# A branch hint for the back edge at the head of every turn of the loops of an image model's kernel

## The reference

```python
out = L0_conv(x)        # 8 heads of 12 channels with rotary positions:
attn = jax.nn.softmax(jnp.einsum('bhnd,bhmd->bhnm', q * scale, k), axis=-1)   # 2304 x 2304 a head
out = jnp.einsum('bhnm,bhmd->bhnd', attn, v)
# L1_conv: a Fourier filter (rfft2, two complex block matrices, irfft2)
# L2_attn: attention with one head of all 192 channels
# L2_ffn:  eight experts, each token to one of them, with a capacity
# L3_attn: retention, 12 heads of 16 channels:
retention = jnp.einsum('mhsd,mhtd->mhst', q, k) * decay
out = jnp.einsum('mhst,mhtd->mhsd', retention, v) + k
# L3_ffn:  jnp.einsum('bsi,oi->bso', x, jnp.sign(weight))
```

## Time and profile before

| | |
|---|---|
| median of 3 runs | 7712.14 us (7709.46 to 7726.1) |
| profiled execution | 7705.95 us |
| its span, first to last instruction | 7704.4 us |
| TensorE matmuls busy | 6614.5 us, 86% |
| VectorE busy | 4720.3 us, 61% |
| ScalarE busy | 3174.2 us, 41% |
| GpSimd busy | 2305.7 us, 30% |
| granted clock of TensorE, mean | 0.907 |

### The profile page before, as it was taken

The page is one execution under the profiler, slowest core; times in us unless marked ns, Lnnn a source line. Parts: engine busy times, 40 slices in busy tenths (PEclk is TensorE's granted clock), DMA queues, the critical chain, the costliest instruction groups (busy, mean ns, idle before and its releaser), DMA issues. The chain is left out here.

```text
span 7704.4 us, 233323 instructions
## 1 busy us (share of the span) xinstructions
PE 6614.5 (86%) x87595; PEld 4183.7 (54%) x87595; DVE 4720.3 (61%) x7714; ACT 3174.2 (41%) x5336; POOL 2305.7 (30%) x2558
## 2 busy tenths in 40 slices
PE   6698999999997677599999982499779999999977
PEld 4254555555554554276767672377445555555546
DVE  6688888888883400132323236011579999999976
ACT  2066666767674133122222220122344444444432
POOL 0011111111111000000000000300339999999961
PEclk8699999999998788699999985799889999999986
DMA  3211111111113423301010012211651111111123
GB/s 116 76 38 38 35 38 36 38 37 38 37 33 79 121 59 92 97 1 28 1 28 19 1 53 83 74 54 42 190 176 37 38 36 37 37 37 38 36 64 105
DMA packets 415540, 428.73 MB, mean 56 GB/s; under 512 B 76977, under 2 KB 387801, under 8 KB 409659
## 3 DMA queue, kind: packets, MB, share of 16 engines
q1 hardware_dynamic: 332859, 339.62, 15.4%
q0 software_dynamic: 62400, 59.16, 3.1%
q10 hardware_dynamic: 19712, 21.53, 0.9%
HBM read 253.47 MB, written 166.55 MB: 55 GB/s over the span
## 5 line engine op out<-in xcount | busy, mean ns | idle before, releaser
L628 DVE TENSOR_REDUCE softmax_part_max<-softmax_ring 128x1 f32<-128x512 f32 (+1 forms) x2880 | 1679.3, 632 | 333.9 <-PE softmax_ring L536 276.2
L2456 POOL TENSOR_TENSOR retention_decayed<-retention_third,retention_decay_table 128x384 f32<-128x384 f32 x1728 | 1690.5, 1005 | 106.1 <-ACT retention_third L2478 101.6
L2437 DVE TENSOR_TENSOR retention_decayed<-retention_scores,retention_decay_table 128x768 f32<-128x768 f32 x1728 | 1654.1, 957 | 89.9 <-PE retention_scores L2398 57.5
L668 ACT ACTIVATE softmax_probs<-softmax_scores 128x768 f32<-128x768 f32 x1728 | 1392.4, 810 | 676.4 <-PE softmax_scores L558 604.1
L536 PE MATMUL softmax_ring<-softmax_k_next,softmax_q_next 96*32 96x512 bf16 (+1 forms) x11520 | 1117.6, 377 | 185.0 <-issue 81.8
L2398 PE MATMUL retention_scores<-retention_q_half,retention_k_piece 96*32 96x384 bf16 x20736 | 1184.8, 325 | 36.6 <-DMA retention_v_piece<-ret_v 29.6
L2478 ACT COPY retention_third<-retention_scores 128x384 f32<-128x384 f32 x1728 | 826.6, 478 | 891.3 <-PE retention_scores L2398 891.3
L2410 PE MATMUL retention_sums<-retention_decayed,retention_v_piece 128*32 128x288 f32 x13824 | 1182.7, 406 | 3.3 <-POOL retention_decayed L2456 0.6
L2398 PEld LDWEIGHTS retention_scores<-retention_q_half,retention_k_piece 96*32 96x32 bf16 x20736 | 628.5, 95 | 516.8 <-DVE retention_decayed L2437 42.4
L569 PE MATMUL softmax_sums<-softmax_probs,softmax_v_piece 128*32 128x192 f32 x13824 | 884.5, 330 | 11.3 <-issue 10.6
L558 PE MATMUL softmax_scores<-softmax_q_third,softmax_k_piece 99*32 99x384 bf16 x13824 | 887.9, 332 | 2.9 <-DMA softmax_v_piece<-rope_v 1.8
(11 more groups left out here) (301 smaller groups left out, 6831.2 us busy)
## 6 DMA issues: line engine op xcount, KB each, us to landing
ret_v<-ret_proj_values SPq DMA_DIRECT2D x8, 1728.0 KB, 8.8
retention_v_piece<-ret_v SPq DMA_DIRECT2D x144, 96.0 KB
softmax_q_third<-rope_q SPq DMA_DIRECT2D x192, 54.0 KB
softmax_q_next<-rope_q POOLq DMA_DIRECT2D x64, 162.0 KB, 3.9
softmax_k_piece<-rope_k SPq DMA_DIRECT2D x192, 54.0 KB
softmax_k_next<-rope_k POOLq DMA_DIRECT2D x64, 162.0 KB, 5.8
ret_q<-ret_proj_parts SPq DMA_DIRECT2D x48, 216.0 KB, 2.8
ret_k<-ret_proj_parts SPq DMA_DIRECT2D x48, 216.0 KB, 3.0
```

Of the source, the lines that this page charges most:

```text
L628: nc.vector.reduce_max(part_max[:, j, c:c + 1], ring[m % 2][:, 0:CHUNKS[c][1]], axis=X)\
L668: nc.scalar.activation(probs[n % 4][:, :].rearrange("p (c q) -> p c q", c=2), scores[n % 2][:, :, 0:QC], ACT.Exp, scale=scale).then_inc(ex ...
L2437: nc.vector.tensor_tensor(weights[n % 4][:, 0:2 * QC].rearrange("p (c q) -> p c q", c=2), scores[n % 2][:, 0:2, 0:QC], table[:, table_at(n ...
L2456: nc.gpsimd.tensor_tensor(weights[n % 4][:, 2 * QC:HALF], third[n % 3][:, :], table[:, at:at + QC], ALU.mult)\
```

## The change

A helper makes the loop of one engine with `hint_back_edge=True`. The framework then puts one more instruction, BRANCH_PREFETCH_HINT, as the first of every turn into that engine's stream. [...] Nothing is added for a loop that runs only once. All else stays.

```diff
+def hinted(nc, eng, start, end):
+
+    return nc.Fori(start, end, engines=bass.OrderedEngineSet([eng.engine]), hint_back_edge=True)
...
     def each_image(self, eng, body):
-        with eng.Fori(0, self.images // 2 - 1) as pair:
+        with hinted(self.nc, eng, 0, self.images // 2 - 1) as pair:
...
-            with sp.Fori(0, n_heads - 1) as h:
+            with hinted(nc, sp, 0, n_heads - 1) as h:
...
-            with pool.Fori(0, n_heads // 2 - 2) as pair:
+            with hinted(nc, pool, 0, n_heads // 2 - 2) as pair:
...
-            with pe.Fori(0, n_heads // 2 - 1) as pair:
+            with hinted(nc, pe, 0, n_heads // 2 - 1) as pair:
...
-            with dve.Fori(0, n_heads) as h:
+            with hinted(nc, dve, 0, n_heads) as h:
...
-            with act.Fori(0, n_heads // GROUP) as group:
+            with hinted(nc, act, 0, n_heads // GROUP) as group:
...
-            with pe.Fori(0, n_heads - 1) as h:
+            with hinted(nc, pe, 0, n_heads - 1) as h:
                 head(h + 1)
```

More of the change, by code:

```diff
@@ L715, in each_image @@
         def each_image(eng, body):
-            with eng.Fori(0, images // 2 - 1) as pair:
+            with hinted(nc, eng, 0, images // 2 - 1) as pair:
                 for i in range(2):
@@ L812, in _ @@
         def _(act):
-            with act.Fori(0, images) as b:
+            with hinted(nc, act, 0, images) as b:
                 for c in range(CH):
@@ L1021, in _ @@
                 sp.dma_start(to, of).then_inc(consts_in, 16)
-            with sp.Fori(0, images) as b:
+            with hinted(nc, sp, 0, images) as b:
                 sp.wait_ge(full, b * USES)
@@ L1031, in _ @@
             pe.wait_ge(negated, 1)
-            with pe.Fori(0, images) as b:
+            with hinted(nc, pe, 0, images) as b:
                 use = [0]
@@ L1175, in _ @@
         def _(dve):
-            with dve.Fori(0, images) as b:
+            with hinted(nc, dve, 0, images) as b:
                 for c in range(CH):
@@ L1331, in _ @@
             sp.dma_start(residual[:, :, :, :], by_rows(x[0, :, :])).then_inc(res_in, 16)
-            with sp.Fori(0, images - 1) as b:
+            with hinted(nc, sp, 0, images - 1) as b:
                 ln.load(sp, b + 1, x[b + 1, :, :])
@@ L1345, in _ @@
             pool.wait_ge(consts_in, 112)
-            with pool.Fori(0, images) as b:
+            with hinted(nc, pool, 0, images) as b:
                 pool.wait_ge(res_in, (b + 1) * 16)
@@ L1530, in _ @@
             ln.normalise(dve, 0, eps)
-            with dve.Fori(0, images - 1) as b:
+            with hinted(nc, dve, 0, images - 1) as b:
                 image(b, True)
@@ L1652, in each_image @@
         def each_image(eng, body):
-            with eng.Fori(0, images - 1) as b:
+            with hinted(nc, eng, 0, images - 1) as b:
                 for c in range(CH):
@@ L2191, in _ @@
             load(1, 1)
-            with sp.Fori(0, E // 2 - 1) as pair:
+            with hinted(nc, sp, 0, E // 2 - 1) as pair:
                 for i in range(2):
@@ L2199, in _ @@
         def _(pool):
-            with pool.Fori(0, E // 2) as pair:
+            with hinted(nc, pool, 0, E // 2) as pair:
                 for i in range(2):
@@ L2243, in _ @@
             pe.wait_ge(ident_in, 16)
-            with pe.Fori(0, E // 2) as pair:
+            with hinted(nc, pe, 0, E // 2) as pair:
                 for i in range(2):
@@ L2256, in _ @@
         def _(act):
-            with act.Fori(0, E // 2) as pair:
+            with hinted(nc, act, 0, E // 2) as pair:
                 for i in range(2):
@@ L2271, in _ @@
         def _(dve):
-            with dve.Fori(0, E // 2) as pair:
+            with hinted(nc, dve, 0, E // 2) as pair:
                 for i in range(2):
@@ L2443, in _ @@
             head(0, first=True)
-            with dve.Fori(0, n_heads - 1) as h:
+            with hinted(nc, dve, 0, n_heads - 1) as h:
                 head(h + 1)
@@ L2460, in _ @@
             head(0, first=True)
-            with pool.Fori(0, n_heads - 1) as h:
+            with hinted(nc, pool, 0, n_heads - 1) as h:
                 head(h + 1)
@@ L2485, in _ @@
             head(0, first=True)
-            with act.Fori(0, n_heads - 1) as h:
+            with hinted(nc, act, 0, n_heads - 1) as h:
                 head(h + 1)
@@ L2600, in _ @@
             add_keys(0, 1)
-            with pool.Fori(0, images - 1) as b:
+            with hinted(nc, pool, 0, images - 1) as b:
                 for rh in range(2):
```

## The result

The changed kernel takes 7739.18 us in the median of 7 runs (7728.73 to 7747.21), the kernel before 7714.28 us (7 runs). The ratio is 1.0031, with a 95% interval of 1.0019 to 1.0042: 25 us slower, where 67 us faster was forecast. On another chip it was 7741.7 against 7713.25 us, 1.0032 (1.0020 to 1.0044). Five executions of all the runs took 10 to 23 ms at a low granted clock (one each of changed_again, slot100_hint, slot100_nohint, fewer_hints and slot170_hint), and the times and ratios here leave them out.

A forecast was written before the change was run, and what follows sets the result against it. Bound taken: instruction-fetch waits at TensorE's softmax back edges. 71 (edges) + 1.5 (wide attention) - 2.7 - 0.8 - 1 (hints) - 1 (exits) = 67 us, profiled 7639, median about 7645 us; range 7603 to 7695 us (0.80).

The forecast's parts named there:

- What bounds the kernel: TensorE's softmax back edges: two instruction-fetch waits (5.8 us) and a slowed clock (1.5 us) cost 7.4 us each, 103 us over 14.
- The first wait: Softmax edge, block with the loop's head: hint fetches it before the branch, which falls from some 3.6 to 0.2 us.
- rival 2: Hint works in part: target comes late or ScalarE's wait shows; half the gain, 33 us, 7679 us; chance 0.07.
- term of 71 us: Saving at TensorE's softmax edges: 5.1 us at each of 14, bounds 59 to 80 us.
- The second wait: Softmax edge, block behind the head's: still fetched late, 2.05 us idle, 1.7 us of it new; bounds 0 and 3.5.
- The clock: TensorE's slow clock behind a softmax edge: 0.6 of its 1.5 us cost stays; bounds 0 and 1.5.
- ScalarE's loop: Softmax loop of four heads: seven issue waits, 25.6 us, hidden beside TensorE's; cost taken as 0, 14 us if its hint failed.
- Wide attention: TensorE's three edges there, 3.2 us idle in all: gain between 0 and 3.2 us, 1.5 taken.
- The cost of a hint: 59 ns a turn: 2.7 us in the retention loop (1.5 to 9.6), 0.8 in softmax, 1 in small loops.
- Leaving a loop: At an exit the block that runs on may be fetched late: 0 to 7.4 us for TensorE's softmax loop, 1 taken.
- Rival 3: The hint, some 4900 instructions ahead of its branch, does nothing; only its cost is left, 7716 us; chance 0.12.
- Rival 4: Retention loop: hints refetch held blocks, pushing out needed ones, some 3.5 us a turn, 161 us more; 7806 us; chance 0.08.

The follow-up runs named there:

- changed_again: The changed kernel, unaltered, measured and profiled once more on another chip: 7741.7 us, ratio 1.0032.
- slot100_hint: Kernel before plus only TensorE's and ScalarE's softmax hints, TensorE's loop head 100 instructions behind a block's start: 7634.1 us, ratio 0.9890.
- slot100_nohint: Kernel before with the head of TensorE's softmax loop 100 instructions behind a block's start, no hints: 7681.02 us, ratio 0.9953.
- fewer_hints: Changed kernel without the five retention-head hints and without VectorE's hint in the token routing: 7722.1 us, ratio 1.0006.
- slot170_hint: Kernel before plus only TensorE's and ScalarE's softmax hints, TensorE's loop head at place 170 of a block: 7683.62 us (one run).
- head_slot0: Kernel before with the head of TensorE's softmax loop at the start of an instruction block, no hints: 7683.63 us, ratio 0.9962.
- ret_tensor_alone: Kernel before with one hint alone, TensorE's on the retention-heads loop: 7718.7 us, ratio 1.0005.

## Why the prediction was wrong

- *What bounds the kernel.* Right. Two waits and the clock make an edge cost 7.4 us, 103 us in all. With both waits gone the softmax stage is 2051.1 us, 99.7 us shorter; the whole kernel gains 85 us by its ratio.
- *The first wait.* This is the step that failed. I wrote "If the hint has the head's block fetched before the branch, it falls", and took the condition as met. By the reading above the block is asked for when the engine is already in the block that holds the branch. Here that is 59 instructions ahead, the packet began 0.6 to 1.0 us behind the branch, and the branch went from 3855 to 3348 ns, and even that came from the edges with two packets. At place 100, where the condition is met, the hint takes the branch from 3610 to 454 ns. I had this as rival 2 ("the branch lies close behind a block's start") with 0.07 and half of the gain. The place could have been counted from the trace before: 38 instructions to the second wait, 5217 a turn, and 2304 from that wait to the one at the sums. The term of 71 us measured some 5 us.
- *The second wait.* That it stays was right, as far as it was put to the test: the first one stayed too. It is the end of the head's block; head_slot0 removed it. The landing was put at 0.25 us: in the retention loop before, the head's first instruction began 0.27 us behind the start of the branch (median of 46). No run shows the term of 1.7 us an edge (2.05 us idle), which takes it that the hint leaves the second fetch as it was. In its place the runs showed a second gap of 1.47 us at the first edge of the changed kernel, behind a first wait of 2.90 us, and at place 100, with the block's end 156 instructions behind the head, none but the 0.36 us for VectorE.
- *The clock.* It stays with the waits (116 us at 0.50 in this loop, 119 before) and goes with them (27 us).
- *ScalarE's loop.* Hidden beside TensorE's, as said. The price if its hint failed, 14 us, was reckoned beside a wait of TensorE's of some 2 us. With none left the same working gives 7 x 3.7 = 26 us; the stage said 32 us and the ratios 25 us.
- *Wide attention.* 1.5 us were forecast, and the stage was 0.8 us longer; one of three branches became short, and none in the second profile. Placed, all three are.
- *The cost of a hint.* The term 46 x 0.059 = 2.7 us measured 0.10 us a turn, 4.7 us, inside its bounds. It is TensorE's hint alone, as said, but more than its own length.
- *Leaving a loop.* The term of 1 us measured 8 us, at a place that I hadn't looked at: VectorE in the routing, where the wait came while the DMA engines' share was 1.00. That the hint says "taken", as two of the expectations put it, is in no trace; that the wait is its doing is shown by the idle instruction in its place, 344.9 against 352.8 us. I had looked at TensorE in the softmax stage, where nothing happened.
- *Rival 3* (no effect, 7716 us) was nearest for TensorE's loop, but missed the exit, and at place 100 the hint was heeded (454 ns against 3610). *Rival 4* named the right stage and a wrong reason: the 16 KB queue moved 449 packets, not 459, and between 5800 and 7440 us, in the retention loop, neither instruction queue moved any.

Of the 25 us, 8 (routing) and 5 (retention turns) are shown by experiments, against some 5 gained. The 6 to 7 us of the Fourier stages are within what kernels without hints there show. What stays open is above all the last stage. Both profiles of the changed kernel have it at 254 to 257 us, at a lower granted clock, longer than in any other. Kernels that keep all its hints there, with a change only in earlier stages, have 240.3, 243.8 and 241.1 us, and ret_tensor_alone, with one hint in all, reached 251.3 us. The 20 us that six hints less give back point to an effect of the changed kernel as a whole. With one or two profiles a kernel I can't tell it from the clock's own spread.

## What to carry to other kernels

A hint on a back edge pays where the closing branch is long (3855 ns in the median here, in a turn of 5217 instructions), and only if the branch stands well behind the start of its block: 98 instructions gave half of the branch back here, 148 nearly all. Count both places, those of the branch and of the loop's head, and move the head; that alone was worth 0.4 to 0.5%, with the hint 1.1%. Leave hints off loops whose branch is short already (208 ns in the retention heads): there they cost about 0.1 us a turn on the engine that the others wait for, and at the exit of the routing loop a wait of 6.67 to 8.07 us.

## What the runs showed of the hardware

- TensorE's taken branch in the softmax loop, in its old place and without a hint, took 3.3 to 4.3 us where one packet of 16 KB began within 2 us behind it, and 4.3 to 5.3 us where two did. With the hint and 198 instructions in the block it took 454 ns. The branch of the retention loop took 208 ns, and from the first of its 47 to the last (5792.6 to 7438.1 us) no instruction packet moved.
- A packet of 16 KB came for every 256 to 262 instructions of TensorE in the softmax loop, and the waits in the middle of turns lay 9 x 256 and, to one instruction, 19 x 256 behind the second wait of the edge (89 and 22 waits in the ten profiles with the loop in its old place).
- A hint that comes in time costs no packet: 315 in place of 329 over the loop, one less at each of 14 edges.
- Behind an edge of the kernel before TensorE's clock was granted at 0.50 for 6.8 to 10.2 us, behind one of head_slot0, with a single wait of 3 us, for 3.4 to 10.2 us. Without the waits it stayed at 1.00 in the first edge's stretch.
- In the kernel before, a group of four matmuls of 384 columns (L558) was followed by the next group 320 ns later at a granted clock of 0.50 (50 of 53 times where that was of L558 too), and 161 to 163 ns later at 1.00 (all 491 times where it was of L536 with 256 columns). These are 1.2 and 2.4 columns a ns, the 1.2 and 2.4 GHz of the prediction.
- A hint of 31 ns on TensorE's sequencer lengthened a retention turn of 35.77 us by 0.10 us.
- In 2 of 18 profiles, those with VectorE's hint in the routing, VectorE stood for 8.07 and 6.67 us in straight code, 32 us behind the loop's exit with the DMA engines' share at 1.00 for the zero fill, and one more instruction packet was moved.
